# Layer norm by blocks inside the LoRA feed-forward, and attention's weights split there into device memory

## The reference

```python
# layer 2: 8 experts, each a LoRA of rank 16 on both matrices, F = 1024; each token takes the best two
h   = layernorm(x)
for each of the two chosen experts e:
    hidden = gelu(h @ W1 + b1 + 2 * (h @ A1[e].T) @ B1[e].T)       # 1024 wide
    out   += weight_e * (hidden @ W2 + b2 + 2 * (hidden @ A2[e].T) @ B2[e].T)
x = x + out
# layer 3: softmax attention over all 2048 tokens, 16 heads of 128; every weight is codes times scales,
# one scale for each block of 32 rows
w = codes * jnp.repeat(scales, 32, axis=0)                          # for wq, wk, wv (256 x 2048), wo (2048 x 256)
q, k, v = layernorm(x) @ wq + bq, layernorm(x) @ wk + bk, layernorm(x) @ wv + bv
x = x + softmax(q k^T / sqrt(128)) v @ wo + bo
```

## Time and profile before

| | us |
|---|---|
| median of 3 runs | 2796.91 |
| lowest and highest run | 2791.83, 2798.86 |
| the profiled execution, device time | 2791.96 |
| its span in the trace | 2790.1 |
| TensorE busy in the span | 2665.0 (96%) |
| VectorE, ScalarE, GpSimd busy | 2050.6 (73%), 1472.9 (53%), 1827.0 (65%) |

### The profile page before, as it was taken

How to read it: one execution, slowest core, us unless ns; L and a number is a source line. 1 busy time by engine, 2 the same in 40 slices (tenths; PEclk the granted TensorE clock), 3 DMA queues, 4 the chain that set the end, 5 groups by cost and what they waited for, 6 DMA issues and landing times. The chain is left out here.

```text
span 2790.1 us, 32396 instructions
## 1 busy us (share of the span) xinstructions
PE 2665.0 (96%) x10762; PEld 1825.2 (65%) x10763; DVE 2050.6 (73%) x3021; ACT 1472.9 (53%) x1837; POOL 1827.0 (65%) x1146
## 2 busy tenths in 40 slices
PE   7886999799999999999999999999999999997998
PEld 2333676567777677777767766776777677764765
DVE  6866434588888888888888888888888888886221
ACT  2323222266666665666666566656656665665122
POOL 2533400367877977787787779778877977785433
PEclk9998899899999999999999999999999999999999
DMA  2001000100000000000000000000000000004621
GB/s 67 0 0 53 0 0 0 39 13 5 16 1 14 12 9 10 7 18 1 14 12 8 7 8 20 1 14 4 16 1 14 8 4 5 1 1 87 233 60 48
DMA packets 58311, 57.90 MB, mean 21 GB/s; under 512 B 8910, under 2 KB 53201, under 8 KB 58162
## 3 DMA queue, kind: packets, MB, share of 16 engines
q1 hardware_dynamic: 55186, 48.79, 6.4%
q0 software_dynamic: 2976, 7.22, 0.9%
HBM read 46.65 MB, written 10.24 MB: 20 GB/s over the span
## 5 line engine op out<-in xcount | busy, mean ns | idle before, releaser
L1706 ACT ACTIVATE at_prob<-at_psum_s 128x1024 f32<-128x1024 f32 x512 | 520.7, 1017 | 642.5 <-PE at_psum_s L919 571.3
L1782 DVE TENSOR_TENSOR at_top<-at_psum_s,at_top 128x512 f32<-128x512 f32 x960 | 662.6, 690 | 169.2 <-ACT at_prob L1706 149.2
L1630 PE MATMUL at_psum_o<-at_prob,at_v 128*128 128x512 f32 x1536 | 703.5, 594 | 2.3 <-issue 1.4
L1771 DVE TENSOR_TENSOR at_prob<-at_prob,at_psum_m 128x1024 f32<-128x1024 f32 x512 | 603.4, 1210 | 0.4 <-PE at_psum_m L1618 0.4
L1946 POOL TENSOR_TENSOR at_acc<-at_acc,at_prob 128x1024 f32<-128x1024 f32 x189 | 449.0, 2376 | 195.6 <-ACT at_prob L1712 194.3
L1712 ACT ACTIVATE at_prob<-at_prob 128x1024 f32<-128x1024 f32 x512 | 536.9, 1049 | 24.3 <-DVE at_prob L1771 24.3
L1950 POOL TENSOR_TENSOR at_acc<-at_acc,at_prob 128x1024 f32<-128x1024 f32 x189 | 456.2, 2414 | 0.0
L1630 PEld LDWEIGHTS at_psum_o<-at_prob,at_v 128*128 128x128 f32 x1536 | 283.2, 190 | 262.1 <-issue 236.7
L917 PE MATMUL at_psum_s<-at_q_hi,sw_gate_up_hi 128*128 128x512 f32 x1024 | 402.4, 393 | 5.3 <-DVE sw_gate_up_lo L1763 5.3
L919 PE MATMUL at_psum_s<-at_q_hi,sw_gate_up_lo 128*128 128x512 f32 x1024 | 401.5, 392 | 0.0
L918 PE MATMUL at_psum_s<-at_q_lo,sw_gate_up_hi 128*128 128x512 f32 x1024 | 400.3, 391 | 0.0
(11 more groups left out here) (349 smaller groups left out, 4400.0 us busy)
## 6 DMA issues: line engine op xcount, KB each, us to landing
ef_gate_up<-in_ef_gate_up SPq DMA_DIRECT2D x8, 1024.0 KB, 14.2
ef_down<-in_ef_down SPq DMA_DIRECT2D x8, 512.0 KB, 14.1
ef_rows_in<-ef_zeros SPq DMA_DIRECT2D x23, 128.5 KB, 8.2
ef_rows<-ef_rows_in SPq DMA_DIRECT2D x23, 128.5 KB, 2.2
x_tok<-in_L_attn_x SPq DMA_DIRECT2D x4, 512.0 KB, 6.9
lf_w<-in_L_ffn_W SPq DMA_DIRECT2D x2, 1024.0 KB, 7.0
at_codes<-in_at_wq_codes SPq DMA_DIRECT2D x16, 128.0 KB, 2.1
at_scales<-in_at_wq_scales SPq DMA_DIRECT2D x64, 32.0 KB, 2.9
```

The costliest lines, as they stand in the source:

```text
L1630: nc.tensor.matmul(psum_o[:], v[:, plain_at[kt], half], prob[u % 2][:, kt, :], start=(c == 0 and t == PAIRED[c]), stop=False)
L1706: nc.scalar.activation(pair(u, c, half), psum_s[:, 2 * half:2 * half + 2, :], ACT.Copy).then_inc(kept, 1)
L1771: nc.vector.tensor_tensor(part, part, psum_m[:].unsqueeze(1).to_broadcast([P, 2, BT]), ALU.subtract).then_inc(shifted, 1)
L1782: nc.vector.tensor_tensor(top[:, u % 2, :], psum_s[:, t, :], top[:, u % 2, :], ALU.max).then_inc(maxed, 1)
```

## The change

**In layer 2's last part** the hardware loops are written out, and three things are added.

1. The layer norm of a block is done inside the next block, by the pieces of `BlockNorm`: statistics at slice 0 on VectorE, the square root at slice 1 on ScalarE, the reciprocal at slice 2, normalizing at slice 3 on ScalarE, the turn (eight transposes) at slice 4 on TensorE, the high part at slice 5, the low part at slice 6. The fourth block's is done in attention's first two steps. `layer_norm_tokens` no longer stands ahead of attention. TensorE no longer waits for the last addition at a block's end.
2. All of attention's weights are split there, in 32 pieces of 256 by 256 in the order q, k, v, o, one piece for each slice of each block. SP loads codes (256 KB) and four transfers of scales into one of two buffers `lf_whole`; GpSimd multiplies them in place (`make_whole`); ScalarE writes the high part (`piece_part`), in its program right behind the slice's two gelus; GpSimd writes the low part (`piece_rest`), in its program behind the product of the following piece; SP stores both parts (512 KB) to device memory and issues the load of the piece two further on.
3. The gelus' output `lf_hidden` has a ring of four slices instead of eight, which makes room.

**In attention** SP loads the high and low parts from device memory with two transfers for each weight, and GpSimd's splits are gone.

```diff
-            hidden = sb("lf_hidden", [P, 2, NF, BT])
+            RING = 4
+            hidden = sb("lf_hidden", [P, 2, RING, BT])
...
+            whole, scales = sb("lf_whole", [P, 2, NC, D]), sb("lf_scales", [P, 2, NC, D])
+            pieces = sb("lf_pieces", [P, 2, 2, NC * D], F32R)
...
+            PIECES = [(name, n) for n in range(8) for name in "qkvo"]
+            N_LOADS = 16 * (1 + NSC)
...
+                @block.sync
+                def _(sp):
+                    def load_piece(p):
...
+                        sp.dma_start(whole[:, p % 2], codes.rearrange("(c p) n -> p c n", p=P)).then_inc(piece_loaded[p % 2], 16)
+                        sc = sc.rearrange("(c q) n -> q c n", q=NSC)
+                        for q in range(NSC):
+                            sp.dma_start(scales[q * BLK:(q + 1) * BLK, p % 2],
+                                         sc[q].partition_broadcast(BLK)).then_inc(piece_loaded[p % 2], 16)
+
+                    def store_piece(p):
+                        name, n = PIECES[p]
+                        sp.dma_start(split_weights[name][n], pieces[:, p % 2].bitcast(F32)).then_inc(piece_stored[p % 2], 16)
+
+                    load_piece(0)
+                    load_piece(1)
+                    for p in range(len(PIECES)):
+                        sp.wait_ge(piece_lo, p + 1)
+                        store_piece(p)
+                        if p + 2 < len(PIECES):
+                            load_piece(p + 2)
+                    for k in range(2):
+                        sp.wait_ge(piece_stored[k], 16 * len(PIECES) // 2)
+
                 @block.gpsimd
                 def _(pool):
+                    def make_whole(p):
+                        pool.wait_ge(piece_loaded[p % 2], N_LOADS * (p // 2 + 1))
+                        nc.gpsimd.tensor_tensor(whole[:, p % 2], whole[:, p % 2], scales[:, p % 2],
+                                                ALU.mult).then_inc(whole_ready, 1)
+
+                    def piece_rest(p):
+                        pool.wait_ge(piece_hi, p + 1)
+                        if p >= 2:
+                            pool.wait_ge(piece_stored[p % 2], 16 * (p // 2))
+                        nc.gpsimd.tensor_tensor(pieces[:, p % 2, 1, :], whole[:, p % 2].rearrange("p c n -> p (c n)"),
+                                                pieces[:, p % 2, 0, :].bitcast(F32), ALU.subtract).then_inc(piece_lo, 1)
...
+                    for p in range(len(PIECES)):
+                        if p % 2 == 0:
+                            add_bias(p // 2)
+                        make_whole(p)
+                        if p >= 1:
+                            piece_rest(p - 1)
+                    piece_rest(len(PIECES) - 1)
...
+                            if b >= 1 and f == 4:
+                                pe.wait_ge(added, b * TPB)
+                                norm.turn(pe, b - 1, rows, turn_psum)
...
-                        pe.wait_ge(added, b * TPB + TPB)
...
+                    def piece_part(p):
+                        act.wait_ge(whole_ready, p + 1)
+                        if p >= 2:
+                            act.wait_ge(piece_stored[p % 2], 16 * (p // 2))
+                        nc.scalar.activation(pieces[:, p % 2, 0, :], whole[:, p % 2].rearrange("p c n -> p (c n)"),
+                                             ACT.Copy).then_inc(piece_hi, 1)
+
+                    for b in range(NB):
                         for f in range(NF):
-                            gelu(0 if f == 0 else 2 * f - 1, f, 0)
-                            gelu(2 * f + 2 if f + 1 < NF else 2 * NF - 1, f, 1)
+                            gelu(b, 0 if f == 0 else 2 * f - 1, f, 0)
+                            gelu(b, 2 * f + 2 if f + 1 < NF else 2 * NF - 1, f, 1)
+                            piece_part(b * NF + f)
+                            if b >= 1 and f == 1:
+                                norm.deviation(act, b - 1)
+                            if b >= 1 and f == 3:
+                                act.wait_ge(d_psum, b * TPB)
+                                norm.normalise(act, b - 1, rows)
+                            if b >= 1 and f == 5:
+                                norm.take_hi(act, b - 1, turn_psum)
```

In attention (the same is done for v and o, and the waits on `w_split`, `wv_split` and `wo_split` become waits on the loads):

```diff
         def load_qk(sp, m, h):
...
+            piece = split_weights["qk"[m]][h // 2].rearrange("p s (c n) -> p s c n", c=NC)
+            for part, to in enumerate((w_hi, w_lo)):
+                sp.dma_start(to[:, m].bitcast(F32), piece[:, part, :, bass.ts(h % 2, HD)]).then_inc(qk_loaded[m], 16)
...
                     for s in range(STEPS):
+                        if s == 1:
+                            first_norm.turn(pe, LAST, first_rows, first_psum)
```

More of the change, by code:

```diff
@@ L1045, in _ @@
                     def _(pool):
+                        nc.gpsimd.memset(norm.eps[:], EPS)
                         pool.wait_ge(split_steps, 3)
@@ L1198, in lora_ffn @@
             biased = semaphore("lf_biased")
-            with nc.Block() as block:
+            piece_loaded = [semaphore(f"lf_piece{k}_loaded") for k in range(2)]
+            whole_ready = semaphore("lf_whole_ready")
+            piece_hi = semaphore("lf_piece_hi")
+            piece_lo = semaphore("lf_piece_lo")
+            piece_stored = [semaphore(f"lf_piece{k}_stored") for k in range(2)]
+            BLK = 32
+            NSC = P // BLK
+            PIECES = [(name, n) for n in range(8) for name in "qkvo"]
@@ new lines, in lora_ffn @@
+            N_LOADS = 16 * (1 + NSC)
+            rows = t2[:].rearrange("p a n -> p (a n)").rearrange("p (j d) -> p j d", j=TPB)
+            turn_psum = [psum_d[:, c, :] for c in range(NC)]
+            norm.begin()
+            with nc.Block() as block:
+                @block.sync
+                def _(sp):
+                    def load_piece(p):
+                        name, n = PIECES[p]
+                        codes, sc = w[f"at_w{name}_codes"], w[f"at_w{name}_scales"]
+                        if name == "o":
+                            codes, sc = codes[n * D:(n + 1) * D], sc[n * NC * NSC:(n + 1) * NC * NSC]
+                        else:
+                            codes, sc = codes[:, n * D:(n + 1) * D], sc[:, n * D:(n + 1) * D]
+                        sp.dma_start(whole[:, p % 2], codes.rearrange("(c p) n -> p c n", p=P)).then_inc(piece_loaded[p % 2], 16)
[4 more added lines that the diff above has]
+                    def store_piece(p):
+                        name, n = PIECES[p]
+                        sp.dma_start(split_weights[name][n], pieces[:, p % 2].bitcast(F32)).then_inc(piece_stored[p % 2], 16)
[8 more added lines that the diff above has]
+                        sp.wait_ge(piece_stored[k], 16 * len(PIECES) // 2)
@@ L1278, in _ @@
                 @block.vector
                 def _(dve):
-                    with dve.Fori(0, NB) as b:
+                    for b in range(NB):
                         tok = bass.ts(b, BT)
@@ L1479, in attention @@
+            for part, to in enumerate((wo_hi, wo_lo)):
+                sp.dma_start(to[:].bitcast(F32), split_weights["o"][h // 2, :, part, bass.ts(h % 2, D)]).then_inc(o_loaded, 16)
+        loaded = semaphore("at_loaded")
         with ExitStack() as inner:
@@ L2093, in expert_ffn @@
             LAST = NB - 1
+            turn_psum = [psum_y[:, c, :] for c in range(NC)]
             def route_bank(b):
@@ L2294, in turn @@
                             pe.wait_ge(ln.lo_copied, norm.copied + NC * b)
-                        norm.turn(pe, b, rows_of[b], psum_y)
+                        norm.turn(pe, b, rows_of[b], turn_psum)
                     def up(b, f):
```

249 lines of the change are left out of this document (107 added, 142 removed).

## The result

| | before | after |
|---|---|---|
| device time, median | 2796.72 us (2791.83 to 2798.86, 4 runs) | 2880.04 us (2874.06 to 2884.74, 4 runs) |
| ratio, 95% interval | | 1.0299 (1.0275 to 1.0324) |
| profiled execution: device time / span | 2791.96 / 2790.1 us | 2877.81 / 2875.7 us |
| layer 2's last part, first matmul to last | 212.7 us | 314.2 us |
| its four blocks | 54.7, 53.0, 53.0, 51.9 | 81.6, 77.9, 78.0, 76.8 |

3.0% slower, as forecast. Plus 101.5, minus 18.1 and plus 4.0 are 87.4. The spans of the profiled executions differ by 85.6: in the changed kernel's the last part began 0.4 us earlier, and what follows attention took 1.5 us less.

The account below looks back on a forecast made before the run. TensorE's own work was taken to bound attention and layer 2's last part. Blocks 95, first loads 4, clock 5, norm's move minus 15 make plus 89 on 2791.96 us, with 2 more 2883; range 2838 to 2935.

Parts of the forecast that it names:

- The chain, 9.5 us forecast: Layer 2's last part: store issue, load, product, low part form one closed chain yielding one piece per C = 9.5 us.
- the transfers as the bound: Rival for layer 2's pieces: the queue falls behind, C is 11 to 12, 2925 to 2950 us; 12 in 100.
- The store in the load: Layer 2's pieces: a 512 KB store ahead of each load costs it 0 to 1.5 us; load taken as 6.2.
- The block, 29.2 + 5C = 76.7: Each block of layer 2's last part: five chain turns count of eight, 76.7 us against 53.0, four times, 95 us.
- The waits, 5 us a slice: Layer 2's last part: TensorE waits some 5 us in most slices and is busy for two thirds.
- The clock, 5 us: TensorE's lower clock behind waits shows in the tails of layer 2's blocks: between 0 and 10 us, taken as 5.
- The norm's move, minus 15: Ahead of attention: the gap falls from 21.7 to 5 us, minus 17, plus 2 in attention; net minus 15.
- 2 us for the last block's norm in attention: Attention's first two steps: the last block's turn, normalizing and high part cost 1 to 3 us, taken as 2.
- What I put at nothing: Three blocks' norm pieces in layer 2, the ring of four gelu tiles, and attention's freed GpSimd: 0 us each.
- a short chain lets the table loads show: Layer 2's last part: with C under about 5, square-root table loads would show, up to 3 us a block.
- Rival 4: GpSimd and VectorE slow each other, products take 1.9 us, not 1.29: C 10.7, 2905 us; within the forecast's 70 in 100.

Follow-up runs that it names:

- low_first: Changed kernel, but GpSimd writes the low part of piece p right behind its product, ahead of the product of p + 1: 2813.78 us, 1.0070 to the kernel before.
- load_first: Changed kernel, but SyncE issues the load of piece p + 2 ahead of the store of piece p: 2853.01 us, 1.0213 to the kernel before.
- spread: both_orders, but with ScalarE's piece copies moved to chosen slices and behind a block's last, bias operations early: 2795.30 us, 1.0003 to the kernel before.
- both_orders: Changed kernel with the edits of load_first and low_first together: 2811.46 us, 1.0066 to the kernel before.
- tail_norm: norm_only, but most norm pieces stand behind the next block's last gelu, with a one-element gelu restoring the table: 2777.11 us, 0.9947 to the kernel before.
- double_store: Changed kernel with each piece stored twice, both stores ahead of the load of p + 2: 2898.61 us, 1.0377 to the kernel before.
- pieces_only: Changed kernel without the norm's move, the layer norm ahead of attention as before: 2893.20 us, 1.0356 to the kernel before.
- norm_only_ring8: norm_only with a ring of eight gelu tiles in place of four: 2789.85 us, 0.9983 to the kernel before.
- norm_only: Kernel before with only the layer norm's move and the ring of four gelu tiles, no weight pieces: 2789.44 us, 0.9985 to the kernel before.

## Why the prediction was right

**The chain, 9.5 us forecast.** It was 9.31 inside the blocks and 9.38 over all steps, and each part has its row above: store with handoff 0.5 forecast, 0.39; load 6.2, 6.49 in the turn shown and 6.45 median; the two GpSimd operations with handoffs 2.8, 2.52. One length for all turns was a simplification: a load took 4.7 to 5.1 us for the output weights, whose scales land in 2.6, and mostly 5.7 to 7.5 for the others. low_first shows that it is this closed chain and not the amount of work: the same operations in another order give two thirds of the loss back. A rival of its kind, the transfers as the bound, falls with load_first and spread, which move the same bytes in a shorter time.

**The store in the load.** I had no row, took 1.1 us of a possible 1.5, and two experiments price it: 1.1 us more load with one store ahead (6.45 against 5.3), 0.6 more with the second (7.1). The Trainium skill (DMA: Bandwidth & Descriptors, Queues, rings and completion order) has descriptors consumed in ring order, by which I had worked out 6.6. The landings agree with it in direction: codes ahead of a store landed in 2.6 us, behind one in 3.5. They don't prove the order, since a store that only shares the way with the load would delay it too, and the price is under the full 1.5 us that I had set for it.

**The block, 29.2 + 5C = 76.7.** Measured 77.9, 78.0, 76.8, and 81.6 for the first, forecast 80.7. The five turns, and not eight, are right: two pieces do get ahead in the down projection. load_first shows the factor too, 6.2 us a block for 1.2 a turn. Part of the closeness is luck, as small errors cancel. In the last three blocks the first low part ended at 7.9 us (7.7 forecast), the turns were 0.2 us shorter than 9.5, which takes 1 us off a block, and what stands behind the copy of the seventh piece took 23.6 to 24.3 us and not 22.2.

**The waits, 5 us a slice.** Right in size, wrong in number. TensorE waits 18 times, 4.0 us on average, not in nearly every slice, 71.6 us in all. The rest is in its busy time: 60.5, 59.8, 60.5 and 61.7 us in the four blocks, 242.5, against 209.3 before, 33.2 more; 24 of the norm's transposes are some 3 us of it, and the rest is mostly matmuls at the lower clock. 71.6 + 33.2, less three waits of 1.10 of before, are 101.5, the loss. Those slow matmuls seem mostly to stand where TensorE would otherwise wait for the chain: only the blocks' tails are longer than the chain accounts for (next point). So TensorE was busy for 77% of the last part, where I had said two thirds, and ScalarE waited for the product as forecast but for TensorE as well.

**The clock, 5 us.** This is what stays of it behind a block's last wait. In the second block, where the granted clock was 0.71 from 429.4 to 437.8 us:

```profile
429.41 0.79 PE L930 MATMUL lf_psum_h<-lf_low_hi,lf_B1T_hi 128*128 128x512 f32 x1 [4.48 <-ACT lf_hidden L1354]
430.00 0.63 PE L931 MATMUL lf_psum_h<-lf_low_lo,lf_B1T_hi 128*128 128x512 f32 x1
430.43 0.63 PE L932 MATMUL lf_psum_h<-lf_low_hi,lf_B1T_lo 128*128 128x512 f32 x1
430.86 6.98 PE L1316 MATMUL lf_psum_t<-lf_hidden,lf_A2T 128*128 128x512 f32 x12
```

Three matmuls 0.43 us apart instead of 0.23 and twelve float32 rows in 6.98 us instead of 5.2: some 2 us in this block. The four tails are 23.6, 24.3, 23.6 and 23.8 us, 6.5 over four times 22.2. No run takes the clock's part away by itself, so 5 or 6.5 stays an estimate.

**The norm's move, minus 15.** It gave 18.1 - 4.0 = 14.1. The gap is 3.6 us and not 5: the first transfer goes out 0.75 us behind the last matmul, the second 0.42 behind that, and it lands in 2.4. The other half, 2 us for the last block's norm in attention, was wrong in kind. both_orders has the changed kernel's attention without any edit, with that work in it, and took 126.0 us to head 1's first score matmul; tail_norm took 126.3, the kernel before 125.8. The same attention program took 126.7 in double_store, 129.4 in load_first and 130.2 in low_first. So the norm's last block costs almost nothing there, and most of the changed kernel's 4.0 us are something that only some executions show. 2.8 of them are one step, behind a wait that both kernels have. In the changed kernel, and then before:

```profile
663.59 0.58 PE L930 MATMUL at_psum_w<-at_wv_hi,x_hi 128*128 128x256 f32 x1 [3.21 <-DVE at_q_lo L1820]
663.97 0.41 PE L931 MATMUL at_psum_w<-at_wv_lo,x_hi 128*128 128x256 f32 x1
664.18 0.41 PE L932 MATMUL at_psum_w<-at_wv_hi,x_lo 128*128 128x256 f32 x1
```

```profile
579.47 0.39 PE L917 MATMUL at_psum_w<-at_wv_hi,x_hi 128*128 128x256 f32 x1 [3.21 <-DVE at_q_lo L1763]
579.69 0.28 PE L918 MATMUL at_psum_w<-at_wv_lo,x_hi 128*128 128x256 f32 x1
579.81 0.28 PE L919 MATMUL at_psum_w<-at_wv_hi,x_lo 128*128 128x256 f32 x1
```

The same wait of 3.21 us, then matmuls 0.21 us apart at a granted clock of 0.50 (663.5 to 669.7 us), and 0.12 apart at 1.00 (579.4 to 583.7 us): 7.1 us from there to the step's first value product instead of 4.2. That the sum of this term came out at 14 is partly luck: a cost that I had at 2 was 0.2 in both_orders, and the lower clock, of which I had counted nothing here, took most of the 4.0.

**What I put at nothing.** The norm's pieces (pieces_only: 313.7 against 314.2), the ring of four (norm_only_ring8), and attention's freed GpSimd (heads 1 to 15 unchanged): all three hold. Of the first, the condition that I gave, a short chain lets the table loads show, is what norm_only shows: the last part is 10 us longer though three waits of 1.10 fell away, so the pieces cost 13, not the 9 in all that "up to 3 us a block" allows.

**Rival 4**, GpSimd's operations stretched by the other engines, did not happen in the changed kernel (median 1.26 us; VectorE stood still during 24 of its 32 products). It did in both_orders, and limits that kernel (last section).

## What to carry to other kernels

Two buffers do not make two pieces in flight: follow the semaphores from a buffer's release to its next release, through each engine's program order, and see what of the other buffer stands in that path. A helper job put in line with work that the bounding engine waits for can cost its latency (2.9 us on ScalarE were 2.29 us of TensorE's wait in norm_only), so it goes where that engine's next need is far off (here behind the last gelu of a block, tables and all). And splitting weights ahead of time bought nothing in a stage whose bound had 1.4 us of waits to give; of this change only the norm's move was worth having, and well placed, with head 0's parts made early, it is 0.7% faster than the kernel before.

## What the runs showed of the hardware that was not expected

- The length of a wait alone does not tell the clock behind it. In the changed kernel TensorE waited 2.80 us three times (385.38, 463.24 and 541.18 us): behind the first two the matmuls were 0.23 us apart, behind the third 0.43. In norm_only three waits of 2.29 us each were followed by half the pace twice, the second time only about 1 us after the wait.
- GpSimd's product of 128x512, the same instruction, takes 1.26 to 1.82 us, and the long ones stand beside VectorE's work. Of the 224 products in the seven profiled kernels with pieces, 101 ran while VectorE stood still, and 17 more beside none of its operations on two SBUF tiles (they ran beside its additions from PSUM, for example): these 118 took 1.26 to 1.30 us. All 58 that took over 1.6 us ran beside an operation of VectorE on two SBUF tiles, for 0.5 us or more. Not every such overlap slowed the product, and no run takes VectorE's work away, so this is shown as what goes together and not as an experiment.
- A store of 512 KB lands in 3.0 us when nothing is ahead of it, and in 4.2 us in load_first, where a load is (medians over all 32 stores).
